# Graph attention and mixture of experts on one core: mask turns in steps of eight, plain row loads, f1 and f2 on two engines, weight split moved

## The reference

```python
# N = 4096 nodes, D = 128, H = 256, E = 8 experts
h = inlayer2 @ W.T + b
f1, f2 = h @ w1 + b1, h @ w2 + b2
logits = f1[:, None] + f2[None, :]
bias = -1e9 * (1.0 - (adj > 0))              # adj: 4096 x 4096 int32
x = x + softmax(leaky_relu(logits, 0.01) + bias) @ layernorm(x)
xn = layernorm(x)
probs = softmax(xn @ gate_w + gate_b)        # the two largest of 8 are kept
for e in range(8):
    y = gelu(xn @ W1[e] + b1[e]) @ W2[e] + b2[e]
    x = x + cw[:, e] * y                      # cw: kept probs, else 0
```

## Time and profile before

| what | value |
|---|---|
| median of three runs | 521.45 us (521.21 to 522.33) |
| the profiled execution | 521.97 us |
| its span | 520.4 us |
| PE busy | 474.6 us, 91% |
| DVE busy | 437.2 us, 84% |
| ACT busy | 211.1 us, 41% |
| POOL busy | 55.1 us, 11% |
| DMA packets | 36432, 44.47 MB; the adjacency queue (q0) 16896 packets |

### The profile page before, as it was taken

One profiled execution on the slowest core, in us unless ns is written; L12 is line 12 of the kernel. 1 busy time (PEld: TensorE's weight loads), 2 busy tenths in 40 slices (PEclk: granted clock), 3 DMA queues, 4 the chain that ended last, 5 costly groups with the idle time before them and its releaser, 6 DMA issues.

```text
span 520.4 us, 5922 instructions
## 1 busy us (share of the span) xinstructions
PE 474.6 (91%) x1760; PEld 232.5 (45%) x1760; DVE 437.2 (84%) x720; ACT 211.1 (41%) x322; POOL 55.1 (11%) x74
## 2 busy tenths in 40 slices
PE   1997879758999999999999999789999999999996
PEld 1976434413444544444444434334434444444442
DVE  0159379999999999999999998397989898988985
ACT  0127400001011110200102114579898888888884
POOL 5000410990200101010000000000000000000000
PEclk9997979789999999999999999979999999999999
DMA  6999999970393975929500000833443575534410
GB/s 132 195 168 117 213 166 147 92 72 1 26 105 33 89 72 46 105 15 104 52 0 0 0 0 9 148 95 66 116 82 101 97 124 110 116 101 101 120 60 22
DMA packets 36432, 44.47 MB, mean 85 GB/s; under 512 B 2320, under 2 KB 24768, under 8 KB 36416
## 3 DMA queue, kind: packets, MB, share of 16 engines
q0 software_dynamic: 16896, 16.78, 34.9%
q1 hardware_dynamic: 18704, 27.46, 22.0%
q10 hardware_dynamic: 816, 0.03, 0.1%
HBM read 92.38 MB, written 2.23 MB: 182 GB/s over the span
## 4 chain that ended last, share of the span: by engine, by line
PE 65%; DVE 16%; issue 7%; DMA 5%; ACT 4%; another core or an unknown queue 1%; SPq 1%; DVEq 1%; ACTq 0%
PE bank L1007 29%; DVE c L804 7%; PE bank L1045 4%; PE bank L1047 4%; PE bank L1046 4%; PE bank L1034 4%; PE bank L1035 4%; PE bank L1036 4%; DMA share<-in_L_gnn_inlayer 2%; PE bank L953 2%; PE bank L945 2%; PE bank L928 2%; DMA share<-shares 2%; ACT mask L544 2%; DVE xs L691 2%
## 5 line engine op out<-in xcount | busy, mean ns | idle before, releaser
L1007 PE MATMUL bank<-c,Y 128*128 128x512 f32 x512 | 234.9, 610 | 18.8 <-DVE c L804 18.7
L804 DVE SCALAR_TENSOR_TENSOR c<-g_row,r_col,maskT 128x512 f32<-128x512 uint8 (+1 forms) x256 | 196.1, 806 | 14.7 <-PE bank L1007 10.7
L1007 PEld LDWEIGHTS bank<-c,Y 128*128 128x128 f32 x512 | 94.5, 193 | 140.9 <-issue 81.5
L847 DVE TENSOR_TENSOR mask<-mask,share 128x1024 f32<-128x1024 f32 x64 | 78.3, 1223 | 23.1 <-ACT mask L544 16.1
L544 ACT ACTIVATE mask<-bank,b1T 128x512 f32<-128x512 f32 x128 | 83.8, 688 | 24.0 <-PE bank L1036 22.4
L853 DVE TENSOR_TENSOR maskT<-mask,maskT 128x1024 f16<-128x1024 f32 x64 | 78.3, 1224 | 0.0
L551 ACT ACTIVATE maskT<-mask 128x1024 f16<-128x1024 f32 x64 | 67.4, 1053 | 4.1 <-DVE mask L847 4.0
L1045 PE MATMUL bank<-maskT,w2h 128*128 128x512 f16 x128 | 49.1, 383 | 6.6 <-DVE maskT L853 6.1
L1035 PE MATMUL bank<-share,w1h 128*128 (+1 forms) x128 | 49.0, 383 | 0.0
L1046 PE MATMUL bank<-maskT,w2h 128*128 128x512 f16 x128 | 49.0, 383 | 0.0
L1047 PE MATMUL bank<-maskT,w2l 128*128 128x512 f16 x128 | 49.0, 383 | 0.0
(11 more groups left out here) (143 smaller groups left out, 343.9 us busy)
## 6 DMA issues: line engine op xcount, KB each, us to landing
mask<-in_adj POOLq DMA_DIRECT2D x32, 512.0 KB, 17.7
share<-shares SPq DMA_DIRECT2D x16, 1024.0 KB, 8.2
share<-in_L_gnn_inlayer SPq DMA_DIRECT2D x8, 256.0 KB, 8.7
share<-in_x SPq DMA_DIRECT2D x8, 256.0 KB, 20.1
out<-c SPq DMA_DIRECT2D x8, 256.0 KB, 3.8
share<-in_L_ffn_W SPq DMA_DIRECT2D x1, 1024.0 KB, 22.0
x<-in_x SPq DMA_DIRECT2D x1, 256.0 KB, 10.1
W_sb<-in_L_gnn_W SPq DMA_DIRECT2D x1, 64.0 KB, 1.9
```

What stands on the lines that cost most here:

```text
L804: dve.scalar_tensor_tensor(c[:, k % CR].rearrange("p (s i) -> p s i", i=32), g_row[:, bass.ds(s * ST, ST)].rearrange("p (s i) -> p s i", i ...
L847: dve.tensor_tensor(hw[:, e % 2], h[:, e % 2], wb[:, e].unsqueeze(1).to_broadcast([P, FC, ST]), ALU.mult).then_inc(hw_done, 1)
L1007: mm(bank[:, par, :], Y[:, k], c[:, k % CR], start=(k == 0), stop=(k == NK - 1)).then_inc(c_used, 1)
```

## The change

Turns read the mask words of a row in steps of eight, so that block b of a turn holds words b, b + 8, b + 16 and on; the node on partition p of block k is then 32 p + k. inlayer2 and x are loaded in that order, which is 128 rows of 16 KB, each tensor in two DMAs of 8 KB per partition. The f1 row matmuls read in2T at a step of 128 elements, and g_row comes out in plain order. f1 and f2 columns of the first 20 blocks stay on PE; those of the last 12 are products and sums on DVE against a broadcast of G. All in2T copies are ScalarE's. Only the first f1 row and 16 of the 32 row sums stand in front of supertile 0; the others follow its mask matmuls. all_rows is made at k = 22. Adjacency 1 is issued when x is in. x2 is one DMA behind the eighth f1 row. W1 and W2 are split by ScalarE (high parts, supertile 1) and DVE (low parts, eight instructions in supertile 2).

```diff
...
+prod = Y
+w_rep = c[:, 2, 0:2 * P].rearrange("p (v d) -> p v d", v=2)
...
+G = c[:, 3, 0:2 * D].rearrange("p (v d) -> p v d", v=2)
...
-def by_chunk(t):
-    return t.rearrange("(q b a e) d -> q a b e d", q=Q, b=NB, a=32, e=4)
...
+by_k = lambda t: t.rearrange("(p k) d -> p k d", p=P)
...
-ROWS = (1, 2, 5, 6, 7, 0)
+ROWS = (1, 2, 5, 6, 7, 4)
+KP = 20
+S_PRE = 16
...
-    for b in (0, half):
-        for q in range(Q):
-            sp.dma_start(dst_k(in2_j, q)[:, b:b + half],
-                         by_chunk(in2)[q].rearrange("a b e d -> a b (e d)")[:, b:b + half]).then_inc(in2_in[b // half], 16)
-    for b in (0, half):
-        for q in range(Q):
-            sp.dma_start(dst_k(x_j, q)[:, b:b + half],
-                         by_chunk(x)[q].rearrange("a b e d -> a b (e d)")[:, b:b + half]).then_inc(xj_in[b // half], 16)
...
+    for n in range(2):
+        part = slice(n * half, (n + 1) * half)
+        sp.dma_start(in2_j[:, part], by_k(in2)[:, part]).then_inc(in2_in[n], 16)
+    for n in range(2):
+        part = slice(n * half, (n + 1) * half)
+        sp.dma_start(x_j[:, part], by_k(x)[:, part]).then_inc(xj_in[n], 16)
...
     sp.wait_ge(f1row_ready, NB)
-    sp.dma_start(x2[:, 0:TS], x_rows[:, 0:TS]).then_inc(xn_in[0], 16)
-    sp.dma_start(x2[:, TS:NK], x_rows[:, TS:NK]).then_inc(xn_in[1], 16)
+    sp.dma_start(x2[:], x.rearrange("(n p) d -> p n d", p=P)).then_inc(xn_in, 16)
+    sp.wait_ge(c_used, NK)
...
-    sp.wait_ge(wsplit, 4)
+    sp.wait_ge(wsplit, 2)
...
     load_adj(0, 0)
+    for n in range(2):
+        pool.wait_ge(xj_in[n], 16)
     load_adj(1, 1)
...
-    def split(raw, hi, lo, arrived=None):
...
-        if arrived is not None:
-            pool.wait_ge(*arrived)
+    def split(raw, hi, lo, done):
...
-        pool.tensor_tensor(lo, raw, hi, ALU.subtract).then_inc(wsplit, 1)
+        pool.tensor_tensor(lo, raw, hi, ALU.subtract).then_inc(done, 1)
...
-    split(gate_sb[:], gate_hl[:, 0:E], gate_hl[:, E:2 * E])
+    split(gate_sb[:], gate_hl[:, 0:E], gate_hl[:, E:2 * E], gate_split)
...
     pool.wait_ge(S_step, 1)
...
     load_adj(2, 0)
-    split(b2_sb[:], b2h[:], b2l[:])
-    pool.wait_ge(wsplit, 2)
+    split(b2_sb[:], b2h[:], b2l[:], S_step)
+    pool.wait_ge(S_step, 4)
...
-    pool.wait_ge(S_step, 5)
+    pool.wait_ge(S_step, 6)
...
     load_adj(3, 1)
-    split(w1raw, w1h[:], w1l[:], arrived=(w_in, 32))
-    split(w2raw, w2h[:], w2l[:])
...
-    for b in range(1, NB, 2):
+    act.wait_ge(dve_const, 1)
+    for b in range(NB):
...
-    act.wait_ge(dve_const, 1)
-    act.wait_ge(bias_ready, 1)
-    act.activation(r_col[:], f2_col[:], ACT.Exp, bias=bias_r[:], scale=-STEEP).then_inc(ru_exp, 1)
-    act.activation(u_col[:], f2_col[:], ACT.Exp, bias=bias_u[:]).then_inc(ru_exp, 1)
-    g_nat = g_row[:, :].rearrange("p (q b a e) -> p b q a e", q=Q, b=NB, a=32, e=4)
-    for b in range(NB):
-        act.wait_ge(f1row_ready, b + 1)
-        act.activation(g_nat[:, b], bank[:, ROWS[b % len(ROWS)], :].rearrange("p (e q a) -> p q a e", e=4, q=Q),
-                       ACT.Exp, bias=bias_g[:], scale=STEEP).then_inc(grow_ready, 1)
...
+    act.wait_ge(bias_ready, 1)
+    act.activation(r_col[:], f2_col[:], ACT.Exp, bias=bias_r[:], scale=-STEEP).then_inc(ru_exp, 1)
+    act.activation(u_col[:], f2_col[:], ACT.Exp, bias=bias_u[:]).then_inc(ru_exp, 1)
...
+    def g_part(b):
+        act.wait_ge(f1row_ready, b + 1)
+        act.activation(g_row[:, ST * b:ST * b + ST], bank[:, ROWS[b % len(ROWS)], :],
+                       ACT.Exp, bias=bias_g[:], scale=STEEP).then_inc(grow_ready, 1)
...
+    g_part(0)
...
+                if p + 1 < NB:
+                    g_part(p + 1)
...
+            if p == 6 and isinstance(s, int) and s == 1:
+                act.wait_ge(w_in, 32)
+                for raw, hi in ((w1raw, w1h[:]), (w2raw, w2h[:])):
+                    act.activation(hi, raw, ACT.Copy, scale=W_SCALE).then_inc(whi_made, 1)
...
-    with act.Fori(0, NS // 2 - 1) as i:
+    supertile(1, 1)
+    supertile(2, 0)
+    with act.Fori(1, NS // 2 - 1) as i:
...
+    for v in range(2):
+        dve.tensor_scalar(w_rep[:, v], ones[:], w_col[:, v:v + 1], None, ALU.mult)
...
-    dve.tensor_copy(G12[:], bank[:, 4, 0:4]).then_inc(g_copied, 1)
-    for b in range(0, NB, 2):
-        dve.wait_ge(in2t_ready, b + 1)
-        dve.tensor_copy(in2T[:, ST * b:ST * b + ST], bank[:, TURN[b % 4], :]).then_inc(in2t_dve, 1)
+    dve.tensor_copy(G, bank[:, 4, 0:2 * D].rearrange("p (v d) -> p v d", v=2)).then_inc(g_copied, 1)
+    dve.tensor_copy(G12[:], bank[:, 4, 2 * D:2 * D + 4]).then_inc(g_copied, 1)
+    dve.wait_ge(g_copied, 2)
+    dve.wait_ge(in2_in[1], 16)
+    dve.tensor_tensor(prod[:, 0:NK - KP], in2_j[:, KP:NK], G[:, 0:1].to_broadcast([P, NK - KP, D]), ALU.mult)
+    link(dve.tensor_tensor(prod[:, NK - KP:2 * (NK - KP)], in2_j[:, KP:NK],
+                           G[:, 1:2].to_broadcast([P, NK - KP, D]), ALU.mult))
+    dve.tensor_reduce(f1_col[:, KP:NK], prod[:, 0:NK - KP], AX_X, ALU.add)
+    link(dve.tensor_reduce(f2_col[:, KP:NK], prod[:, NK - KP:2 * (NK - KP)], AX_X, ALU.add))
...
-    dve.wait_ge(g_copied, 1)
...
-    mask32 = mask[:].rearrange("p r s j -> p r (s j)").bitcast(U32)
+    mask32 = mask[:].rearrange("p r s j -> p r (s j)").bitcast(U32).rearrange("p r (s w b) -> p r s b w", s=PS_, w=32)
...
     def turn(n, p, par):
...
-        dve.transpose(at32v[:, par, PS_ * p:PS_ * p + PS_, :].rearrange("p s w -> p (s w)"),
+        dve.transpose(at32v[:, par, PS_ * p:PS_ * p + PS_, :].rearrange("p s (b w) -> p s b w", b=NB),
...
-    dve.wait_ge(xj_in[0], 64)
-    stats(0, B1)
+    for n in range(2):
+        dve.wait_ge(xj_in[n], 16)
+        last = stats(n * B1, (n + 1) * B1)
+    link(last)
+    for k in range(NK):
+        ins = dve.bn_aggr(mv1[:, k], st1[:, k])
+    ins.then_inc(mv1_ready, 1)
...
-    f12 = bank[:, 4, 2 * P:2 * P + 2 * NK].rearrange("p (k v) -> p v k", v=2)
-    dve.tensor_copy(f1_col[:], f12[:, 0])
-    dve.tensor_copy(f2_col[:], f12[:, 1])
-    link(dve.tensor_scalar(nf2[:], f12[:, 1], -1.0, None, ALU.mult))
+    f12 = bank[:, 4, 2 * D + 32:2 * D + 32 + 2 * KP].rearrange("p (k v) -> p v k", v=2)
+    dve.tensor_copy(f1_col[:, 0:KP], f12[:, 0])
+    link(dve.tensor_copy(f2_col[:, 0:KP], f12[:, 1]))
+    link(dve.tensor_scalar(nf2[:], f2_col[:], -1.0, None, ALU.mult))
...
-    dve.wait_ge(xj_in[1], 64)
-    link(stats(B1, NK))
-    for k in range(NK):
-        ins = dve.bn_aggr(mv1[:, k], st1[:, k])
-    ins.then_inc(mv1_ready, 1)
-    for p in range(2):
-        turn(1, p, 0)
+    dve.wait_ge(sd1_ready, 1)
+    dve.reciprocal(rs1[:], sd1[:]).then_inc(rs1_ready, 1)
...
-    dve.wait_ge(sd1_ready, 1)
-    dve.reciprocal(rs1[:], sd1[:]).then_inc(rs1_ready, 1)
...
-    for p in range(2, NP):
+    for p in range(NP):
...
-            if first and k == 0:
-                dve.wait_ge(grow_ready, NB)
+            if k == 0:
+                dve.wait_ge(grow_ready, 1 if first else NB)
...
-                dve.wait_ge(xn_in[0], 16)
-                dve.wait_ge(xn_in[1], 16)
+                dve.wait_ge(xn_in, 16)
...
-            if first and k == 4:
+            if first and k == S_PRE + 6:
...
+            if isinstance(s, int) and s == 2 and k % 3 == 0 and k < 24:
+                v, cols = k // 12, slice(k // 3 % 4 * 512, k // 3 % 4 * 512 + 512)
+                flat = [(w1raw, w1h, w1l), (w2raw, w2h, w2l)][v]
+                raw, hi, lo = (w.rearrange("p a b -> p (a b)")[:, cols] for w in (flat[0], flat[1][:], flat[2][:]))
+                dve.wait_ge(whi_made, v + 1)
+                ins = dve.scalar_tensor_tensor(lo, raw, W_SCALE, hi, ALU.mult, ALU.subtract)
+                if k % 12 == 9:
+                    ins.then_inc(wsplit, 1)
...
-    with dve.Fori(0, NS // 2 - 1) as i:
+    supertile(1, 1, 2)
+    supertile(2, 0, 2)
+    with dve.Fori(1, NS // 2 - 1) as i:
...
-    mm(bank[:, 4, 0:2], W_sb[:], w_col[:], start=True, stop=True)
-    mm(bank[:, 4, 2:4], b_rep, w_col[:], start=True, stop=True).then_inc(gc_done, 1)
+    for v in range(2):
+        mm(bank[:, 4, D * v:D * v + D], w_rep[:, v], W_sb[:], start=True, stop=True)
+    mm(bank[:, 4, 2 * D:2 * D + 2], W_sb[:], w_col[:], start=True, stop=True)
+    mm(bank[:, 4, 2 * D + 2:2 * D + 4], b_rep, w_col[:], start=True, stop=True).then_inc(gc_done, 1)
...
-        pe.wait_ge(in2_in[b // (NB // 2)], 64)
-        need(pe, in2t_act if b % 2 else in2t_dve, (b - 2) // 2)
+        pe.wait_ge(in2_in[b // (NB // 2)], 16)
+        need(pe, in2t_act, b - 3)
...
-        pe.wait_ge(in2t_act if b % 2 else in2t_dve, b // 2 + 1)
+        pe.wait_ge(in2t_act, b + 1)
...
-            ins = mm(bank[:, 4, 2 * P + 2 * k:2 * P + 2 * k + 2], in2T[:, P * k:P * k + P], G12[:, 0:2],
+            ins = mm(bank[:, 4, 2 * D + 32 + 2 * k:2 * D + 34 + 2 * k], in2T[:, P * k:P * k + P], G12[:, 0:2],
...
+    FB = KP // 4
...
-            pe.wait_ge(g_copied, 1)
-        if b >= 2:
-            f_cols(b - 2)
-    f_cols(NB - 2)
```

(34 more changed lines are left out.)

## The result

The changed kernel took 539.11 us (median of four runs, 537.61 to 539.85), the kernel before, on the same chip, 521.75 (521.21 to 522.33): a ratio of 1.0329 (95%: 1.0303 to 1.0354). The forecast was 525.8. The direction was right, and so were most of the times forecast up to the end of supertile 1, some of them by luck, as the part on the prediction shows; the size was not, +17.4 against +4.3. The profiled execution took 539.09 us, span 537.5.

A forecast was written before the change was run, and what follows sets the result against it. It took the start as bound by the DMA engines and settled supertiles by nearly full PE and DVE. Cumulative change: -0.8 after supertile 0, +0.4 after 1, +4.3 after 2; 521.5 + 4.3 = 525.8 us, 8-in-10 range 517 to 547.

The forecast's parts named there:

- Turns: DVE turns reading mask words 32 B apart: no change, 1.24 us each; upper bound twice, +1.1 each.
- Rival B: Strided turns are slow, +1.1 us each, 2.9 per settled supertile, sum 21: 547; chance 20%.
- the f1 matmul ..., I take 0: f1 rows on PE reading in2T at 512 B steps: bounds 0 to 0.86 us each, taken as 0.
- Adjacency 2: Issued at 80.9 behind all_rows, beside x2, landing at 112.2; supertile 1's turn waits over 12 us, end 138.4.
- The 1.6 us for the last receipt: Term at the end of adjacency 2's load, 1.6 us, within its landing at 112.2.
- the forecast case: Whole kernel: adjacency 2 stall replaces GpSimd's splits, strided reads cost nothing; 525.8 us, own range 520 to 531, chance 45%.
- The start: Up to supertile 0's end: x at 22, first pass 43.6, adj 1 at 59, supertile 0 ends at 90.4.
- rival C: At the start, 8 KB rows travel as 2 KB packets, x lands at 36, total 530; chance 10%.
- the early first pass would be lost behind adj 1: Supertile 0: PE's first pass gains 12 us, not kept, since the turn before k=8 needs adj 1.
- The bytes stay, so the last byte of adj 1 moves little by this: Loads at the start: 16 DMAs becoming 4 of 8 KB rows hardly move adj 1; x2's move gives 6.0 us.
- Weight split: Eight low-part products on DVE in supertile 2: 5.5 minus 1.4 us of slack, +4.1; bounds 2 to 5.5.
- Rival A: Supertile 1: adjacency 2 lands below 108, the stall is shorter, GpSimd's gain outweighs the DVE split: 517; chance 25%.

The follow-up runs named there:

- e6: Kernel before with only the weight split moved off GpSimd (high parts ScalarE in supertile 1, low parts DVE in supertile 2): 509.09 us.
- e9: Kernel before with the weight split moved, x2 loaded after adjacency 1, and low-part products spread two each over supertiles 2 to 5: 508.72 us.
- e11: As e2, with the f1 rows read contiguously too: 521.47 us.
- e2: Changed kernel with only the turn's reading put back to neighbouring mask words: 520.71 us.
- e4: Kernel before with only the node order, strided turns and f1 rows, and 8 KB row loads: 533.14 us.
- e3: Kernel before with its four turns at 4, 8, 16 and 32 byte steps and f1 rows at several steps: 528.74 us, one run.
- e1: Changed kernel with old node order, 2 KB row loads, contiguous turns and f1 rows, four f1 rows in front of supertile 0: 528.89 us.

## Why the prediction was wrong

**The step that failed is "Turns", "I take no change".** Of the two bounds, 1.24 and +1.1, the rows show 2.02: +0.78 for each of 32. The row it was drawn from was the wrong neighbour: ScalarE reading PSUM (685 ns at 512-byte steps, 688 contiguous) is another engine and another memory than DVE reading SBUF. That equality holds as measured, and says nothing about SBUF. No row of before had a strided 4-byte read by DVE, so the two ends were open; and DVE had no cover, which the prediction said itself. Rival B, at 20%, was the case: the strided turns are slow (2.02 us) and little covers them; its settled price of 2.9 was 2.6, and its 21 us measured 18.7. That these lie so close is partly luck. A turn costs 0.78 more and not the 1.1 of its sum, and with 0.78 and the 1.4 us of slack that it takes off, a settled supertile would pay 1.7 and the whole 14 us; the turns found only 0.5 of that slack. DVE's slack of the earlier trace rows is no fixed allowance: the weight split found 1.6 of its 5.4 us (e6), the spread products 0.2 of 1.4 (e9).

**The same failure, hidden: "the f1 matmul ..., I take 0".** A pass took 0.85 instead of 0.43, the upper end. It costs 2.8 us in supertile 0 and nothing in the time (e11), because adj 2's issue, and with it the landing, moves by no more than 0.2 us.

**Adjacency 2 was right.** Forecast and trace: issue 80.9 and 79.9, x2 at 87.0 and 89.3, turn at 112.2 and 110.0, a wait of "over 12 us" and 13.1, end of supertile 1 at 138.4 and 138.6. The queue's rows between 96 and 100 us of the kernel after show about as many packets of x2 as of adj 2, as forecast (packets, MB, share of the engines' time):

```profile
q0 software_dynamic: 261, 0.26, 68.9%
q1 hardware_dynamic: 263, 0.54, 39.4%
```

The 1.6 us for the last receipt in the landing at 112.2 is an estimate of mine that no run shows: in the kernel after, GpSimd's queue moves the last packet of adj 1 between 57.0 and 57.2 us, and the turn that waits for the tile starts at 57.45.

But the end at 138.6 agrees partly by luck. With contiguous turns it is 134.4 (e2): adj 2 landed 4 us earlier than forecast (its issue at 77.9 instead of 80.9 is 3 of them), and slow turns gave 4 back. For the same reason the forecast case itself, 525.8, was 5 too high; e2 measures it at 520.7. The terms are these 4 us and the 1.8 us by which the part behind supertile 2 is shorter, and both lie inside the forecast's own range of 520 to 531.

**The start was right in its times, and in part by luck.** x at 22 as the 8 KB packet would have it, so rival C falls; between 12 and 14 us of the kernel after:

```profile
q1 hardware_dynamic: 73, 0.47, 58.5%
q0 software_dynamic: 76, 0.08, 40.9%
```

0.47 MB in 73 packets is 6.4 KB on average. Of the 224 packets of all queues in those 2 us 167 are under 8 KB; the other 57, at 8 KB each, are the whole 0.47 MB. Adj 1 at 57.4 (59), supertile 0 at 92.7 (90.4, the turns being 2.0 of the difference). That the early first pass would be lost behind adj 1 came true. Two steps behind these times failed. "The bytes stay, so the last byte of adj 1 moves little by this": e4, where x2 stays beside the tile, moves it by 5.1 us, 3.0 of it being engine time that the larger rows save. And without the slow turns supertile 0 ends at 90.65 (e2), as forecast, only because the f1 rows, put at 0, gave back 2.8 us; with both reads contiguous it ends at 87.8 (e11).

**Weight split.** +4.1 in supertile 2 measured 3.8 (e6). Rival A, that the GpSimd gain outlives the late transfer, needed a landing by 108. It came at 110 in the changed kernel and at 108 in e2, which is on the point, and e2 sums to nothing, as A's condition has it.

## What to carry to other kernels

Before an access order is traded for larger DMA rows, work out the byte step at which every engine will read: here 4-byte reads 16 or 32 bytes apart cost VectorE 63% (2.02 us for 1.24), reads 8 bytes apart nothing (1.23), and 512 bytes apart they doubled a TensorE pass (0.85 us for 0.43). On an engine that is as full as the bound, that price repeats in every stage (here 2.6 us in each settled supertile, e2), whereas what the DMAs win comes once (3.0 us of engine time, e4), and may be hidden behind the next transfer. When a step moves later, look at what is queued behind it on the engine that waits for it; here one DMA issue behind a small wait ate all of a 12 us gain.

## What the runs showed of the hardware

- The turn has two durations only, 1.24 us at 4 and 8 bytes and 2.02 at 16 and 32 (e3).
- An f32 pass of 512 columns from SBUF takes 0.43 us contiguous, 0.92 at 32-byte steps and 0.85 at 512-byte steps (e3), while the ScalarE read of PSUM at 512-byte steps took 685 ns and an instruction of the same size that reads PSUM contiguously 688.
- In two stretches of the kernel after, the queues of SP and GpSimd moved nearly equal numbers of packets: 73 to 76 between 12 and 14 us, with 8 KB rows on SP's, and 263 to 261 between 96 and 100 us, with 2 KB packets. The queue with 8 KB rows moved 0.47 MB in its 2 us, the other 0.08.
- Plain loads of 4.2 MB take 14.0 us of engine time in 2 KB rows and 10.7 in 8 KB rows (e4).
- GpSimd has long gaps around its all-reduce, with nothing in the profile that it waits for. In e1 the all-reduce starts 10.1 us after the end of an adjacency issue, 6.9 us after its inputs are ready, and the next instruction comes another 10.5 us later; in the kernel before that one comes 7.5 us after the all-reduce. The issue alone doesn't do it: there a plain instruction starts at 63.67, right behind the issue at 60.86, which lasts 2.78 us. The cause is open.
